# Attention of a two-layer block: the order of matmuls between score pairs, the bank of the value projection, and four units for a batch's stores

## The reference, cut to what matters

```
q = query @ W_Query + B_Query          # 256 -> 1024 = 16 heads x 64
k = key @ W_Key + B_Key
v = value @ W_Value + B_Value
scores = einsum('bqhd,bkhd->bhqk', q, k) / D ** 0.5
probs = softmax(scores, axis=-1)
out = einsum('bhqk,bkhd->bqhd', probs, v)
return out.reshape(B, Lq, H * D) @ W_Output + B_Output
```

## Time and profile before

| what | value |
|---|---|
| timed runs, median (lowest to highest of 3) | 1724.06 us (1721.96 to 1731.62) |
| the profiled execution's own time | 1734.78 us |
| its span, first to last instruction | 1733.1 us |
| mean granted TensorE clock over the span | 0.942 |
| TensorE matmuls, busy | 1555.7 us (90%), 22101 records |
| TensorE weight loads, busy | 986.8 us (57%), 22101 records |
| VectorE, busy | 1139.6 us (66%) |
| ScalarE, busy | 722.9 us (42%) |
| GpSimd, busy | 600.3 us (35%) |

### The profile page before, as it was taken

The page is one execution under the profiler, slowest core; times in us unless marked ns, Lnnn a source line. Parts: engine busy times, 40 slices in busy tenths (PEclk is TensorE's granted clock), DMA queues, the critical chain, the costliest instruction groups (busy, mean ns, idle before and its releaser), DMA issues. The chain is left out here.

```text
span 1733.1 us, 51974 instructions
## 1 busy us (share of the span) xinstructions
PE 1555.7 (90%) x22101; PEld 986.8 (57%) x22101; DVE 1139.6 (66%) x2625; ACT 722.9 (42%) x1678; POOL 600.3 (35%) x730
## 2 busy tenths in 40 slices
PE   6569999998799999999999999999999999953583
PEld 4356777776355565656656565665655656543352
DVE  6434656552477777787777777777677778748770
ACT  3324444432344454445454454545455444412120
POOL 2133445441233332333333333333333233310585
PEclk9759999999799999999999999999999999965797
DMA  8200000000533334234333324334243334322254
GB/s 249 50 13 13 14 24 1 1 0 1 149 82 75 93 77 104 70 87 112 69 92 89 93 70 112 78 79 117 63 93 100 81 81 100 88 71 63 59 84 56
DMA packets 94664, 127.92 MB, mean 74 GB/s; under 512 B 19424, under 2 KB 51424, under 8 KB 94432
## 3 DMA queue, kind: packets, MB, share of 16 engines
q1 hardware_dynamic: 88288, 116.07, 26.5%
q0 software_dynamic: 6144, 8.52, 3.2%
HBM read 94.95 MB, written 29.62 MB: 72 GB/s over the span
## 5 line engine op out<-in xcount | busy, mean ns | idle before, releaser
L1131 POOL TENSOR_SCALAR at_Pr<-at_Pr,at_rinv 128x512 f32<-128x512 f32 x512 | 348.2, 692 | 725.2 <-DVE at_rinv L1149 725.2
L1092 ACT ACTIVATE at_Pr<-at_ps,at_nmax 128x512 f32<-128x512 f32 x512 | 347.5, 684 | 390.0 <-DVE at_nmax L1142 390.0
L1156 DVE STREAM_TRANSPOSE at_blocks<-at_Pr 128x512 f32<-128x512 f32 x512 | 360.8, 705 | 87.3 <-POOL at_Pr L1131 87.3
L1142 DVE TENSOR_REDUCE at_nmax<-at_ps 128x1 f32<-128x512 f32 x512 | 329.0, 684 | 132.1 <-PE at_ps L966 130.9
L979 PEld LDWEIGHTS at_ps<-at_blocks,at_V 32*64 32x64 f32 x16384 | 247.5, 131 | 142.1 <-issue 130.3
L979 PE MATMUL at_ps<-at_blocks,at_V 32*64 32x128 f32 x16384 | 297.9, 278 | 8.3 <-issue 6.7
L966 PE MATMUL at_ps<-at_k,at_q 64*128 64x512 f32 x1024 | 289.0, 641 | 4.3 <-ACT at_Pr L1092 4.1
L966 PEld LDWEIGHTS at_ps<-at_k,at_q 64*128 64x128 f32 x1024 | 77.1, 184 | 120.1 <-ACT at_Pr L1092 102.2
L992 PE MATMUL at_ps<-at_wo,at_oT 128*128 128x256 f32 x512 | 129.4, 396 | 1.7 <-ACT at_oT L1074 1.6
L992 PEld LDWEIGHTS at_ps<-at_wo,at_oT 128*128 128x128 f32 x512 | 93.1, 192 | 59.7 <-issue 46.2
L938 PE MATMUL at_ps<-m_ctxT,at_w_rest 128*128 128x512 f32 x224 | 120.4, 619 | 0.1
(11 more groups left out here) (231 smaller groups left out, 1670.8 us busy)
## 6 DMA issues: line engine op xcount, KB each, us to landing
at_V<-spread_v SPq DMA_DIRECT2D x256, 256.0 KB, 4.6
spread_v<-at_V SPq DMA_DIRECT2D x64, 256.0 KB, 2.1
k_x<-in_x SPq DMA_DIRECT2D x8, 512.0 KB, 8.6
mg_ctx<-in_ctx SPq DMA_DIRECT2D x8, 512.0 KB, 9.0
mx_ctxn<-in_ctx SPq DMA_DIRECT2D x8, 512.0 KB, 3.7
rows<-m_ctxT SPq DMA_DIRECT2D x16, 256.0 KB, 5.6
out<-k_x SPq DMA_DIRECT2D x8, 512.0 KB, 6.9
r_w<-in_L_ffn_w SPq DMA_DIRECT2D x16, 256.0 KB, 5.4
```

Source lines behind the costliest of these rows:

```text
L1092: act.activation(Pr[:, n % P_RING, :], bank(n), ACT.Exp, bias=nmax[:, at], accum_out=rsum[:, at]).then_inc(s["exp"], 1)
L1131: pool.tensor_scalar(Pr[:, at, :], Pr[:, at, :], rinv[:, at:at + 1], 1.0, ALU.mult, ALU.mult).then_inc(s["pn"], 1)
L1142: dve.tensor_reduce(nmax[:, n % P_RING:n % P_RING + 1], bank(n), AX.X, ALU.max, negate=True).then_inc(s["nmax"], 1)
L1156: dve.transpose(blocks[:, u % 2, h, :, m, :], Pr[:, n % P_RING, :].rearrange("p (n q) -> p n q", n=KB)).then_inc(s["blocks"], 1)
```

## The change

TensorE's order within a unit becomes: slot 0, half of q of u+1, the output of u-2, the other half of q; slot 1, the first half of PV of u-1; slot 2, transposes or gate logits if there are any, then v of u+1, then k of u+1; slot 3, the second half of PV of u-1. v is written to the score bank that tile 6 of unit u will take (slot 3); so it waits for an exponential of slot 1, and the score pair of slot 3 waits for ScalarE's copy of v. ScalarE moves the head output ahead of slot 0's exponentials, the copy of v between the two exponentials of slot 2, the copy of k to slot 3 and the copies of transposes and logits to slot 2. VectorE adds the output in slot 0 instead of slot 1. `store_rows` becomes four DMAs of 256 KB, one in each of units 4 to 7.

```
-    PV_PARTS = ((2, 0, KB // 2), (3, KB // 2, 3 * KB // 4), (0, 3 * KB // 4, KB))
+    VALUES_AT = TILES - 2
+        def values_bank(u):
+            return bank(TILES * (u - 1) + VALUES_AT)
-        NORM, APPLY, TURN, GATE, LAST = 2, 3, 4, 6, B - 1
+        NORM, APPLY, TURN, STORE, GATE, LAST = 2, 3, 4, 4, 6, B - 1
@@ SyncE
-                def store_rows(b):
-                    sp.wait_ge(s["xn"], b + 1)
+                def store_rows(b, d):
+                    if d == 0:
+                        sp.wait_ge(s["xn"], b + 1)
...
+                def store_x(b, half):
+                    ov = out[0:N, :].rearrange("(b k h p) d -> b p k h d", k=2, h=2, p=P)
+                    at = b * TPB + 2 * half
+                    sp.dma_start(ov[b, :, half, :, :], x_all[:, at:at + 2, :]).then_inc(landed, 16)
...
                 for u in range(U):
                     spread_values(u)
-                    if routed(u, TURN) is not None:
-                        store_rows(routed(u, TURN))
-                store_rows(LAST)
+                    for part in range(2):
+                        if routed(u, STORE + part) is not None:
+                            store_rows(routed(u, STORE + part), part)
+                        if routed(u, STORE + 2 + part) is not None:
+                            store_x(routed(u, STORE + 2 + part), part)
...
@@ TensorE: project
-                        wait_count(pe, s["V"], u)
+                        wait_count(pe, s["k"], u)
                         pe.wait_ge(s["scaled"], min(u + 1, 2))
                     elif d == 0:
                         pe.wait_ge(s["q"], u + 1)
+                        for r in range(DC):
+                            if routed(u - 1, TURN + r) is not None:
+                                pe.wait_ge(s["xT"], DC * routed(u - 1, TURN + r) + r + 1)
+                        if routed(u - 1, GATE) is not None:
+                            pe.wait_ge(s["lg"], routed(u - 1, GATE) + 1)
@@ TensorE: project_values
-                    pe.wait_ge(s["k"], u + 1)
...
+                    wait_count(pe, s["exp"], TILES * (u - 1) + VALUES_AT - S_RING + 1)
                     for t in range(TPB):
                         for d in range(DC):
-                            ins = pe.matmul(ps[:, A_BANK, P * t:P * t + P],
+                            ins = pe.matmul(values_bank(u)[:, P * t:P * t + P],
@@ TensorE: score
+                        if u == 0:
+                            pe.wait_ge(s["V"], 1)
+                    if 2 * m == VALUES_AT:
+                        pe.wait_ge(s["V"], min(u + 2, U))
@@ TensorE: the loop, behind score(u, m)
+                        if m == 0:
+                            if there(u + 1):
+                                project(u + 1, 0, 0)
+                            if there(u - 2):
+                                output(u - 2, 0)
+                                output(u - 2, 1)
+                            if there(u + 1):
+                                project(u + 1, 0, 1)
+                        if m == 1 and there(u - 1):
+                            weigh_values(u - 1, 0, KB // 2)
-                        if m == 3 and there(u):
+                        if m == 2 and there(u):
                             if any(routed(u, r) is not None for r in (TURN, TURN + 1, GATE)):
-                                pe.wait_ge(s["k"], u + 2)
+                                pe.wait_ge(s["q"], u + 2)
...
-                        if m == 3 and there(u + 1):
+                        if m == 2 and there(u + 1):
                             project_values(u + 1)
+                            project(u + 1, 1, 0)
+                            project(u + 1, 1, 1)
+                        if m == 3 and there(u - 1):
+                            weigh_values(u - 1, KB // 2, KB)
@@ ScalarE
+                values(0)
                 for u in range(U + 2):
                     for m in range(SLOTS):
+                        if m == 0 and there(u - 2):
+                            heads_out(u - 2)
+                        if m == 2 and there(u):
                             for d in range(DC):
                                 if routed(u, TURN + d) is not None:
                                     keep_rows(routed(u, TURN + d), d)
...
+                        if m == 3 and there(u + 1):
+                            keys(u + 1)
                         if there(u):
+                            weights_of(u, m, 0)
+                        if m == 2 and there(u + 1):
+                            values(u + 1)
+                        if there(u):
+                            weights_of(u, m, 1)
                         if m == 0 and there(u + 1):
                             queries(u + 1)
@@ VectorE
-                        if m == 1 and there(u - 2):
+                        if m == 0 and there(u - 2):
                             add_out(u - 2, 0)
...
@@ experts, GpSimd
-                pool.wait_ge(landed, 16 * (B + 1))
+                pool.wait_ge(landed, 16 * (2 * B + 1))
```

More of the change, by code:

```diff
@@ L923, in _ @@
                     spread_values(u)
-                    if routed(u, TURN) is not None:
-                        store_rows(routed(u, TURN))
-                store_rows(LAST)
+                    for part in range(2):
[3 more added lines that the diff above has]
+                            store_x(routed(u, STORE + 2 + part), part)
+                for part in range(2):
+                    store_rows(LAST, part)
+                for part in range(2):
+                    store_x(LAST, part)
             @block.tensor
@@ L1024, in _ @@
                             score(u, m)
-                        if m == 1 and there(u - 2):
-                            output(u - 2, 0)
-                            output(u - 2, 1)
-                        if m == 1 and there(u + 1):
-                            project(u + 1, 1, 0)
-                        if m == 2 and there(u + 1):
-                            project(u + 1, 1, 1)
-                        if m == 3 and there(u):
+                        if m == 0:
[9 more added lines that the diff above has]
+                        if m == 2 and there(u):
                             if any(routed(u, r) is not None for r in (TURN, TURN + 1, GATE)):
-                                pe.wait_ge(s["k"], u + 2)
+                                pe.wait_ge(s["q"], u + 2)
                             for d in range(DC):
@@ L1039, in _ @@
                                 map_gates(routed(u, GATE))
-                        for slot, first_block, last_block in PV_PARTS:
-                            if m == slot and there(u - 1 - (slot == 0)):
-                                weigh_values(u - 1 - (slot == 0), first_block, last_block)
-                        if m == 0 and there(u + 1):
-                            project(u + 1, 0, 0)
-                            project(u + 1, 0, 1)
-                        if m == 3 and there(u + 1):
-                            project_values(u + 1)
-                pe.wait_ge(s["V"], U)
+                        if m == 2 and there(u + 1):
+                            project_values(u + 1)
+                            project(u + 1, 1, 0)
+                            project(u + 1, 1, 1)
+                        if m == 3 and there(u - 1):
+                            weigh_values(u - 1, KB // 2, KB)
+                pe.wait_ge(s["k"], U)
                 for d in range(DC):
@@ L1067, in values @@
                     wait_count(act, s["v_out"], 16 * (u - 1))
-                    act.copy(V[:, u % 2, :, :], ps[:, A_BANK, :].rearrange("p (t d) -> p t d", t=TPB)
+                    act.copy(V[:, u % 2, :, :], values_bank(u).rearrange("p (t d) -> p t d", t=TPB)
                              ).then_inc(s["V"], 1)
@@ L1097, in _ @@
                 keys(0)
+                values(0)
                 for u in range(U + 2):
                     for m in range(SLOTS):
-                        if m == 0 and there(u):
-                            values(u)
-                        if m == 3 and there(u):
+                        if m == 0 and there(u - 2):
+                            heads_out(u - 2)
+                        if m == 2 and there(u):
                             for d in range(DC):
@@ L1107, in _ @@
                                 keep_logits(routed(u, GATE))
+                        if m == 3 and there(u + 1):
+                            keys(u + 1)
                         if there(u):
-                            for h in range(2):
-                                weights_of(u, m, h)
-                        if m == 0 and there(u - 2):
-                            heads_out(u - 2)
+                            weights_of(u, m, 0)
[3 more added lines that the diff above has]
+                            weights_of(u, m, 1)
                         if m == 0 and there(u + 1):
                             queries(u + 1)
-                        if m == 2 and there(u + 1):
```

(1 more changed line is left out.)

12 lines of the change are left out of this document (2 added, 10 removed).

## The result

| | median us (runs) | ratio to before, 95% interval | profiled execution, its span | clock |
|---|---|---|---|---|
| before | 1725.03 (1721.96 to 1731.62) | 1 | 1734.78, 1733.1 | .942 |
| after | 1684.73 (1682.58 to 1687.19) | 0.976 [0.974, 0.978] | 1682.58, 1680.8 | .949 |

A forecast was written before the change was run, and what follows sets the result against it. TensorE, busy throughout a 16.27 us unit, was taken to set the pace. Matmul order -41.5, instruction supply -8 and edges +1 sum to -48.5, from 1724.06 to 1675 us; bounds 1664 to 1686, range with rival 1 1664 to 1705.

The forecast's parts named there:

- Order of the matmuls: TensorE's loop units: fewer changes of kind remove fixed parts, 0.68 us a unit over 61 units, -41.5 us.
- Transposes and gate maps: Moved from slot 3 to slot 2 with the same records; claimed to cost 0.
- Rival 1: TensorE's fixed part belongs to each operation, not to each change of kind: 1701 us, chance 0.12.
- The ring: Score banks awaiting exponentials: slots 1 and 3 shrink to 3.08 us, 0.38 us of cover is left, cost 0.
- The new waits: Waits on V's copy, slot 1's exponential, the head output, additions and spread values: all in time, cost 0.
- Instruction supply: TensorE's instruction packets: stretching of the 64-record PV in slot 3 mostly goes, -8 us, bounds -11 and 0.
- Rival 3: Instruction supply starves both 128-record PV blocks of a unit, making the kernel slower: 1751 us, chance 0.05.
- Stores: Four 256 KB DMAs over four units instead of 1 MB in one: 0, any gain counted under instruction supply.
- Edges: First score waits for V's copy, units 0, 1 and 63 lack fillers: +1 us, from -1 to +3.
- The clock: TensorE's granted clock in the loop stays at 1.00, the 2.4 GHz level; falling below would prove the prediction wrong.
- The level: Sum -48.5 us: profiled execution 1734.78 to 1686.3; from the timed runs' median, 1724.06, to 1675 us.

The follow-up runs named there:

- e2: Changed kernel with K's second half moved between two halves of slot 3's PV, ScalarE's copy of K behind slot 3's exponentials: 1706.94 us, ratio 0.989.
- e3: Changed kernel with the value projection back in the bank that Q and K share: 1771.59 us, ratio 1.026 to before.
- the second profile: Changed kernel run and profiled again, unaltered: 1684.92 us, ratio 0.975 to before.
- e5: Changed kernel with idle TensorE instructions, placed so that in every second unit a packet begins 4 instructions ahead of slot 1's PV: 1741.78 us, ratio 1.008.
- e10: Changed kernel with idle TensorE instructions between V and K, packet borders 20 or 148 instructions ahead of slot 1's PV: 1721.35 us, ratio 0.996.
- e1: Changed kernel with a finished batch's four store DMAs issued in one unit again: 1688.97 us, ratio 0.977 to before.
- e11: Kernel of e10 with a batch's four stores also issued together in one unit: 1719.91 us, ratio 0.996 to before.
- e12: Changed kernel with idle TensorE instructions behind long matmuls (14 behind K, up to 14 behind Q's first half): 1708.96 us, ratio 0.988.

## Why the prediction held, and where it did not

**Order of the matmuls, -41.5: held.** 0.64 us a unit instead of 0.68 (the two full-array slots came 0.01 and 0.02 over, PV 0.01 over), 61 x 0.64 = -39.0. Transposes and gate maps, which the forecast had at 0, gave 3.4 more (21.4 to 18.0 in all), since a value projection right behind them shares their fixed part too. Rival 1 is out by the timeline and by e2. The Trainium skill, TensorEngine Tiling (Array Packing), Key Properties, has the rule that a change of mode drains the engine and a change of tile does not; Q, output and Q in 3.64, where three fixed parts would make 4.05, agree.

**The ring, 0: held.** Cover 0.36 us measured, 0.38 worked out; no score of units 2 to 62 waits for an exponential. **The new waits, 0: held** but for the 0.6 us of two PV blocks, with e3 as what the old bank would have cost.

**Instruction supply, -8: failed.** The waits grew, from 9.3 us to 13.7 (11.5 in the second profile). The first fault is in the reading of the rows: of the 8.8 us counted there, 2.2 lie in the three stretches at clock 0.50 and are no waits for instructions. The second is the step from "128 records pass that fast only where a packet begins at a PV" to "so the waits mostly go". The waits of the 64-record PV did go. But the step treated the packet's arrival as a matter of how fast the packet before it runs, and did not ask what else decides when it leaves, the transfers on the engines among it. V was moved, and its write moved with it, to 2 us ahead of a PV of 128; the prediction counted the load of the spread values and the stores, but not the write. Its own row had the sign: at 658.60 in the earlier trace rows the wait followed a burst of stores. In that case the packet starts at 656.25, close to the end of 2 MB that leave from 648.64 to 656.77. In before most late packets follow a packet that ran in 3 to 4 us, as the step had it; in after most start at the end of a transfer. Rival 3's mechanism (a PV of 128 that isn't fed in time) is real, in 17 blocks of 122 and not in all; e5 shows it at 49 us of stretched blocks. The Trainium skill, Runtime: NRT & Kernel Launch, Instruction fetch mechanics, has blocks of 256 instructions, the next fetched while the present one runs; the runs agree. That this hides the fetch they do not bear out: none to 49 us of 1000 by the border's place alone (e10, e5).

**Stores, 0: nearly.** Together they made one packet later, the wait on it longer, and the clock fall behind it, 4.9 us in all (e1), and they cost nothing where no packet is needed soon (e11). The forecast had at most 1.59, one wait out of eight batches.

**Edges, +1:** within the spread of the edges, 7 us on either side, nothing can be told.

**The clock,** which the forecast had at 1.00 in the loop, gave 2.9 us: three stretches at 0.50 in before, one in after. That is luck, as far as the runs show: the runs of the changed kernel with one edit have none to seven of them between the marks.

**The level.** -39.0 - 3.4 + 4.4 (waits) + 0.6 - 2.9 (clock) is -40.3 for the 61 units, with -0.8 in unit 1 -41.1 where -41.2 were measured between the marks; the forecast had -49.5, too much by the -8 that did not come. From 1724.06, -41.2 would have given 1682.9; measured 1684.73. That 1686.3, forecast for the profiled execution, lies close to its 1682.58 is chance: that pair differs by 11 us at the edges and by the level of before's run.

What stays open: no run moved or removed the transfers of values alone, so that they delay the packets rests on the times in all runs and on e1, where added stores lengthened one wait. In the changed kernel eight of the twelve packets at the write are late before the write begins, so their cause is open. That the write's end matters is seen in e3, where the write ends about 1 us earlier against slot 3's scores and the packets start as much earlier. Why the packet of e12 is sent for after the load has begun, and that of e10 before it, with the border at one place, was not settled either. A version faster than the changed kernel was not found.

## What to carry to other kernels

Count the changes of kind between neighbouring matmuls, price one from two sizes of the same piece in the timeline, and put work of one kind together if a free bank lets it stand there; the price held to within 0.04 us a unit. A step that is moved takes its transfers with it: look what they run against, the instruction queue included. Before a stretched row is put down to a wait, read the granted clock of that stretch. A test that adds work to an engine must put it behind the wait that matters, or it runs in idle time and shows nothing.

## What the runs showed of the hardware

TensorE's instructions come in packets of 256 (174 for 44628). Where a row waited for a packet, it ran 2.2 us or more after the packet's transfer started. A packet usually starts 0.6 to 1.0 us after the packet ahead of it begins to run. Under the 1 MB load of values, or at the end of their 256 KB write, it starts up to 4.6 us after, and a block of 128 small matmuls, which passes 256 instructions in 2 us, then stands for 0.3 to 1.9 us, 3.2 with the stores on top.

Idle instructions on TensorE's queue are free behind 512-column matmuls (14 at a time: K to scores 1.81, Q to output 0.96 in e12) and cost 1.2 us for 28 behind 128-column ones (V to K 3.1 instead of 1.89 in e10).

The granted clock fell from 1.00 to 0.50 for a few microseconds at a time inside a loop whose mean reads 1.00 or 0.99: behind a wait of 3.21 us in e1, and at some gate maps (one of seven in after, three of seven in e1, none in e10). V behind gate maps then takes 3.35 us to the next piece instead of 1.87.
